# Routed expert blocks of 128 slots become pairs of 64-slot units, each with its own expert, in two column halves of the array

## The chip, the core and the metric

The kernel runs on one NeuronCore of one Trainium2 chip. Its engines each have an instruction queue of their own: TensorE (PE, matmuls; PEld its weight loads), VectorE (DVE), ScalarE (ACT), GpSimd (POOL) and SyncE (SP). SP computes nothing here: it issues nearly all DMA transfers, in program order. Engines wait for each other through semaphores. The metric is the device time of one execution in microseconds (us).

## The reference, cut to what matters

Two layers work on x, 1024 tokens of 256 features. Each adds a gated cross attention to x and then a gated mixture of experts. The attention does not change here. The mixture of experts is

```
x1       = layernorm(x)
combine  = top-k of 32 experts per token, with weights  # layer 0: 8 of 32, hidden width 176; layer 1: 6 of 32, width 96
routed   = sum over experts e: combine[:, e] * ((silu(x1 @ Wg[e]) * (x1 @ Wu[e])) @ Wd[e])
shared   = (silu(x1 @ sWg) * (x1 @ sWu)) @ sWd
x        = x + tanh(g) * (routed + shared)
```

All of it is in 32-bit floats. Only a token's own 8 (or 6) experts are computed: 8192 pairs of token and expert in layer 0, 6144 in layer 1.

## The kernel before, in words

**Routing.** VectorE finds for every token its experts and its place in each expert's segment of a DRAM buffer, `xs_dram` (32 segments). GpSimd scatters the normed rows there with indirect DMAs (L1723). Each segment is read in blocks of 128 slots. How full an expert gets is known only at run time, so the program holds a fixed number of blocks that is enough in the worst case, `BLOCKS` (L59): 95 in layer 0 and 79 in layer 1. `tables` (L1436) writes two rows of numbers for them into `tab`: where each block starts in `xs_dram`, and which expert it belongs to.

**One routed block**, in the order of its data:

1. SP loads the block's 128 rows into `xs` (L759), a ring of 8 buffers. In layer 0 it also loads the expert's down weights with two DMAs (L765), into `dn`, a ring of 8 buffers that lie in `oT` and `osb_v`. Start row and expert are read from `tab` into SP's registers four blocks at a time (`table_of`, L742 and L746).
2. PE transposes the rows (L948), and ACT copies them to `xTs` (L1199).
3. PE multiplies by the expert's gate and up weights (L982: contraction 256 in two halves, 352 output columns in layer 0, 192 in layer 1). All experts' gate and up weights lie in `W`, and a register picks the expert (`expert_in`, L956).
4. ACT applies silu (L1208), DVE multiplies (L1489), PE transposes the product (L994), DVE copies it to `hT` (L1500).
5. PE multiplies by the down weights (L1015). In layer 1 all down weights lie in `dn1`, next to the gate and up weights, and the expert is again picked by a register.
6. ACT scales the result (L1218), GpSimd scatters it to DRAM (L1733). To which row each slot goes, DVE works out for four blocks at a time (`goes_to`, L1502 to L1524).

A matmul of 32-bit floats shows as two instructions in the trace. The loop (`ffn` on each engine) is written out by hand: in step q PE transposes block q+1, multiplies gate and up of block q, transposes h of block q-1 and multiplies down of block q-2; a block has no loop counter at run time, every instruction is written out.

**Before and after.** Ahead of each layer's routed blocks stand 8 tiles of the shared expert (24 and 16 units in the same loop). SP starts the routed loads when all scatters have landed, and behind the last block it waits for all y scatters and reads the sums.

Of the kernel before, what the change touches and what calls it, by code (L numbers as in the profile page):

```python
# [21 lines left out]
P = 128  # L22
# [36 lines left out]
BLOCKS = tuple((T * k + EXPERTS * (P - 1)) // P for k in TOP)  # L59
# [4 lines left out]
XS_RING, Y_RING, Y2_RING, IDX, IDX_RING = 8, 4, 4, 4, 16  # L64
# [14 lines left out]
def build(nc, a):  # L79

    ctx = ExitStack()
    with ctx:
# [71 lines left out]
        junk = sb("junk", [P, 3, EXPERTS])  # L154
        bv = sb("bv", [P, 12])
        tab = sb("tab", [1, 2, 96], I32)
# [8 lines left out]
        row_no = sb("row_no", [P, 1])  # L165
        expert_no = sb("expert_no", [P, EXPERTS])
# [34 lines left out]
        with ExitStack() as prep:  # L201
# [18 lines left out]
        dn = [v[0:88, i * 2 * D:(i + 1) * 2 * D].rearrange("p (c n) -> p c n", c=2)  # L220
              for v in (oT[:, :, :].rearrange("p k t -> p (k t)"), osb_v[:, :]) for i in range(XS_RING // 2)]
# [8 lines left out]
        Wv = [W[:, 0:n * 2 * D].rearrange("p (j k g e r) -> p k g j e r", j=n, k=KD, g=2, e=EXPERTS) for n in (44, 24)]  # L230
        dn1 = W[0:96, 24 * 2 * D:24 * 2 * D + EXPERTS * D].rearrange("p (e n) -> p e n", e=EXPERTS)
# [81 lines left out]
        with nc.Block() as block:  # L313
            @block.sync
            def _(sp):
# [15 lines left out]
                for layer in range(2):  # L331
                    sp.dma_start(xs_dram[layer].rearrange("(e s) n -> s e n", s=SEG)[0:P],
                                 zeros[:, :].unsqueeze(1).to_broadcast([P, EXPERTS, ROW])).then_inc(padded[layer], 16)

            @block.gpsimd
            def _(pool):
# [33 lines left out]
                for layer in range(2):  # L370
                    k = TOP[layer]
                    pool.iota(token_row[:, layer, :], pattern=[[P * k, NT]], base=-1, channel_multiplier=k, **small)
                    step(pool.iota(dump_row[:, layer, :], pattern=[[P, Y_RING]], base=T * k, channel_multiplier=1, **small))
# [300 lines left out]
        def scatters(layer, u):  # L674
# [14 lines left out]
        dn_in = [sem(f"dn_in{i}") for i in range(XS_RING)]  # L689
# [3 lines left out]
            "xT_ps", "xT_sb", "g_ps", "s", "h", "hT_ps", "hT_sb", "down", "y_ps", "y_sb", "x_sh", "idx", "half", "pe_sum", "sum")}  # L693
# [15 lines left out]
        def all_scattered(layer, slot):  # L709

            return 16 * (len(range(slot, BLOCKS[0], Y_RING)) + layer * len(range(slot, BLOCKS[1], Y_RING)))

# [6 lines left out]
        with nc.Block() as block:  # L719
            @block.sync  # L720
            def _(sp):
# [17 lines left out]
                def table_of(layer, b):  # L739

                    n = min(IDX, BLOCKS[layer] - b)
                    _, rows = nc.values_load_multi_w_load_instructions(  # L742
                        tab[0:1, 0, b:b + n], engines=(mybir.EngineType.SP,), min_val=0, max_val=EXPERTS * SEG - P)
                    if layer == 1:
                        return [(r, None) for r in rows]
                    _, experts = nc.values_load_multi_w_load_instructions(  # L746
                        tab[0:1, 1, b:b + n], engines=(mybir.EngineType.SP,), min_val=0, max_val=EXPERTS - 1)
                    return list(zip(rows, experts))

                def block_in(layer, b, row, expert):  # L750
# [8 lines left out]
                    sp.dma_start(xs[:, slot, :], xs_dram[layer][bass.DynSlice(row, P), :]).then_inc(xs_in[slot], 16)  # L759
                    if layer == 0:  # L760
                        if b >= XS_RING:
                            sp.wait_ge(cf["down"], unit_of_block(b - XS_RING) + 1)
                        rows = wffn[0][SHARED[0]:, :, 2 * D:].rearrange("j (e c s) n -> j e c s n", e=EXPERTS, s=2)
                        for half in range(2):
                            sp.dma_start(dn[slot][half * TILES[0]:(half + 1) * TILES[0], :, :],  # L765
                                         rows[:, bass.DynSlice(expert, 1), :, half, :].rearrange("j e c n -> j (e c) n")
                                         ).then_inc(dn_in[slot], 16)

                def blocks_in(layer):

                    sp.wait_ge(cp["tab"], layer + 1)
                    table = table_of(layer, 0)
                    sp.wait_ge(scattered[layer], 16 * NT * TOP[layer])
                    for b in range(BLOCKS[layer]):
                        if b and b % IDX == 0:
                            table = table_of(layer, b)
                        block_in(layer, b, *table[b % IDX])
# [54 lines left out]
            def _(pe):  # L832
# [93 lines left out]
                def spread(layer):  # L926
# [5 lines left out]
                    for i in range(4):  # L932
                        last = pe.matmul(bank(7)[:, i * P:i * P + nb], rep[:, i, :], ident[:, 0:nb], start=True, stop=True)
                    last.then_inc(cp["rep_ps"], 1)

                def x_block_transposed(q):
# [4 lines left out]
                    pe.wait_ge(xs_in[slot], 16 * ring_turn(layer, b, XS_RING))  # L941
# [9 lines left out]
                def expert_in(q):  # L951

                    layer, _, b, _ = units[q]
                    if b == 0:
                        pe.wait_ge(cp["tab"], layer + 1)
                    _, of_block[q] = nc.values_load_multi_w_load_instructions(  # L956
                        tab[0:1, 1, b:b + 1], engines=(mybir.EngineType.PE,), min_val=0, max_val=EXPERTS - 1)

                def gate_up(q):
# [12 lines left out]
                    else:  # L972
# [7 lines left out]
                        pe.wait_ge(cf["xT_sb"], n + 1)  # L980
                        for k in range(KD):
                            last = pe.matmul(out, xTs[:, n % 2, k, :],  # L982
                                             Wv[layer][:, k, :, :, bass.DynSlice(of_block[q][0], 1), :],
                                             start=k == 0, stop=k == KD - 1)
# [12 lines left out]
                def down(q):  # L997
# [8 lines left out]
                    if kind == "routed" and layer == 0:  # L1006
                        pe.wait_ge(dn_in[index % XS_RING], 32 * (index // XS_RING + 1))
                    for c in range(parts):
                        if kind == "shared":
                            w = sw[:, part, 2 * D:]  # L1010
                        elif layer == 0:
                            w = dn[index % XS_RING][:, c, :]
                        else:
                            w = dn1[:, bass.DynSlice(of_block[q][0], 1), :].rearrange("p e n -> p (e n)")
                        last = pe.matmul(out, hT[0:rows, q % 2, c * P:(c + 1) * P], w, start=part == 0 and c == 0,  # L1015
                                         stop=ends(q) and c == parts - 1)
# [296 lines left out]
            def _(dve):  # L1313
# [122 lines left out]
                def tables(part, layer):  # L1436

                    nb = BLOCKS[layer]
                    if part == 0:
# [3 lines left out]
                        step(dve.tensor_scalar(nblk[:, :], count[:, :], 1.0 / P, 63.5 / P, ALU.mult, ALU.add))  # L1443
                        step(dve.tensor_scalar(nblk[:, :], nblk[:, :], ROUND, ROUND, ALU.add, ALU.subtract))
                        step(dve.tensor_tensor_scan(endb[:, :], ones[:, 0:EXPERTS], nblk[:, :], 0.0, ALU.mult, ALU.add))
                        before_it, own_count, nth, latest, rows = [bv[:, i:i + 1] for i in range(5)]
                        start, inside = bv[:, 5:6], bv[:, 6:7]
                        expert, lower, upper, row = [bv[:, i:i + 1] for i in range(8, 12)]
                        dve.scalar_tensor_tensor(junk[:, 0, :], endb[:, :], row_no[:, :], nblk[:, :], ALU.is_le, ALU.mult,
                                                 accum_out=before_it)  # L1450
                        step(dve.scalar_tensor_tensor(junk[:, 1, :], endb[:, :], row_no[:, :], ones[:, 0:EXPERTS], ALU.is_le,
                                                      ALU.mult, accum_out=expert))
                        dve.scalar_tensor_tensor(junk[:, 2, :], expert_no[:, :], expert, count[:, :], ALU.is_equal, ALU.mult,
                                                 accum_out=own_count)
                        dve.tensor_scalar(inside, expert, EXPERTS - 1.0, float(SEG), ALU.min, ALU.mult)
                        step(dve.tensor_scalar(nth, before_it, row_no[:, :], -1.0, ALU.subtract, ALU.mult))
                        dve.tensor_scalar(latest, own_count, -float(P), 0.0, ALU.add, ALU.max)
                        step(dve.tensor_scalar(rows, nth, float(P), None, ALU.mult))
# [4 lines left out]
                        dve.tensor_copy(rep[:, :, :], bv[:, 8:12].unsqueeze(2).to_broadcast([P, 4, P])).then_inc(cp["rep"], 1)  # L1463
                    else:
                        dve.wait_ge(cp["rep_ps"], layer + 1)
                        ps = bank(7)
                        dve.tensor_copy(tab[0:1, 0, 0:nb], ps[0:1, 3 * P:3 * P + nb])
                        dve.tensor_scalar(tab[0:1, 1, 0:nb], ps[0:1, 0:nb], EXPERTS - 1.0, None, ALU.min)
# [4 lines left out]
                        step(dve.tensor_scalar(low[:, 0:nb], ps[:, P:P + nb], row_no[:, :], None, ALU.is_le))  # L1473
                        dve.scalar_tensor_tensor(filled[:, 0:nb], ps[:, 2 * P:2 * P + nb], row_no[:, :], low[:, 0:nb],
# [26 lines left out]

                def goes_to(layer, b, part):  # L1502
# [7 lines left out]
                    elif part == 1:  # L1510
                        for i in range(b, b + n):
                            dve.wait_ge(xs_in[i % XS_RING], 16 * ring_turn(layer, i, XS_RING))
# [20 lines left out]
                def ffn(layer, i):  # L1533
# [85 lines left out]

                for s in range(STEPS):  # L1620
# [264 lines left out]
```

## Time and profile before

| | |
|---|---|
| time, median of 3 runs | 890.02 us (890.01 to 892.17) |
| span of the profiled execution, from its first to its last instruction | 931.3 us |
| routed blocks of layer 0, first gate matmul to last down matmul | 352.5 to 595.4 us |
| routed blocks of layer 1, the same | 762.3 to 902 us |
| busy share of the span: PE, DVE, ACT, POOL | 80%, 58%, 47%, 52% |

The profiled execution was longer than the timed ones; nothing is given of what lies around its span. The rows of its trace are shown further down. In them, PE, DVE, ACT and POOL rows are instructions at work, and SPq rows are DMA issues in SP's queue.
### The profile page before, as it was taken

Reading aid. Unit: us, or ns where it says so; the run is one execution under the profiler, and the core shown is the slowest. Engines: PE = TensorE matmul, PEld = TensorE weight load, DVE = VectorE, ACT = ScalarE, POOL = GpSimd, SP = SyncE. Lnnn points to the kernel's source line nnn. Section 1 sums busy time; section 2 is a strip of 40 time slices with the busy share of each in tenths; the row PEclk is TensorE's granted clock in tenths of the full one; section 3 lists DMA queues with packets and bytes.
Section 4 is the critical chain, followed back from the end, with each engine's and each line's share of the span. In section 5 each row is a group of like instructions: output and inputs, shape, how many; then the busy total and the mean of one; then the engine's idle time right before and its main releaser. Section 6 shows DMA issues by size and latency. Waiting matters only on the chain.

```text
span 931.3 us, 20204 instructions
## 1 busy us (share of the span) xinstructions
PE 741.2 (80%) x5678; PEld 544.3 (58%) x5719; DVE 535.8 (58%) x1323; ACT 437.5 (47%) x1058; POOL 480.9 (52%) x530
## 2 busy tenths in 40 slices
PE   6657777767687878999999999548856579999974
PEld 4535455544455665677777777425545467777753
DVE  5989879789784533344344444277653444444435
ACT  3568776666663112444444444236633015555540
POOL 3817665787886551333433433375246535555550
PEclk9869875775857798999999999857877789999997
DMA  8909999999999945656666666378026435555538
GB/s 281 371 10 184 172 164 193 177 216 216 202 187 248 331 159 174 189 182 198 197 188 199 191 187 198 138 281 299 16 77 176 152 114 180 167 171 172 159 108 313
DMA packets 222085, 175.53 MB, mean 188 GB/s; under 512 B 146698, under 2 KB 200922, under 8 KB 220954
## 3 DMA queue, kind: packets, MB, share of 16 engines
q1 hardware_dynamic: 207978, 132.52, 56.2%
q0 software_dynamic: 13728, 41.17, 12.3%
q8 instruction: 52, 0.85, 0.4%
q14 instruction: 55, 0.45, 0.2%
q10 hardware_dynamic: 272, 0.52, 0.1%
HBM read 87.92 MB, written 52.69 MB: 151 GB/s over the span
## 4 chain that ended last, share of the span: by engine, by line
PE 42%; issue 11%; POOL 11%; DVE 11%; DMA 10%; ACT 3%; SPq 3%; another core or an unknown queue 2%; POOLq 0%; DVEq 0%; ACTq 0%
PE psum L982 15%; PE psum L1015 11%; DMA pT<-p 6%; POOL p L1710 3%; POOL xs_dram L1723 3%; PE psum L994 3%; DVE nmax L1321 3%; PE psum L948 3%; POOL y_dram L1733 3%; PE psum L970 2%; DMA W<-y_dram 2%; PE psum L841 2%; ACT e L1169 1%; SPq L765 1%
## 5 line engine op out<-in xcount | busy, mean ns | idle before, releaser
L1733 POOL DMA_INDIRECT y_dram<-ybuf,idxi x174 | 167.4, 962 | 232.7 <-ACT ybuf L1218 186.7
L1500 DVE COPY hT<-psum 88x256 f32<-88x256 f32 (+2 forms) x214 | 74.2, 347 | 214.6 <-PE psum L994 103.0
L982 PE MATMUL psum<-W,xTs 128*128 x696 | 196.0, 405 | 0.7 <-issue 0.7
L1169 ACT ACTIVATE e<-psum,nmax 128x1024 f32<-128x1024 f32 x128 | 142.4, 1115 | 57.6 <-DVE nmax L1321 40.6
L1710 POOL TENSOR_SCALAR p<-e 128x1024 f16<-128x1024 f32 x128 | 133.9, 1046 | 65.6 <-ACT e L1169 38.9
L1321 DVE TENSOR_REDUCE nmax<-psum 128x1 f32<-128x1024 f32 x128 | 152.3, 1219 | 20.5 <-PE psum L841 17.3
L1723 POOL DMA_INDIRECT xs_dram<-xaug,posi x112 | 110.3, 985 | 69.2 <-issue 31.9
L1208 ACT ACTIVATE sg<-psum 128x176 f32<-128x176 f32 (+2 forms) x214 | 61.1, 286 | 161.9 <-PE psum L982 82.4
L1218 ACT ACTIVATE ybuf<-psum,dot 128x256 f32<-128x256 f32 x174 | 82.6, 474 | 110.3 <-PE psum L1015 100.9
L982 PEld LDWEIGHTS psum<-W,xTs 128*128 128x128 f32 x696 | 115.9, 193 | 23.2 <-issue 2.9
L841 PE MATMUL psum<-kstack,qstack 128*128 128x512 bf16 x215 | 93.2, 511 | 40.4 <-ACT e L1169 33.2
L854 PEld LDWEIGHTS psum<-osb_v,pT 128*128 128x128 f16 x1024 | 66.7, 104 | 53.5 <-DMA pT<-p 37.9
L994 PE MATMUL psum<-ident,h 128*88 128x128 f32 (+2 forms) x309 | 71.2, 281 | 23.4 <-DVE h L1492 12.3
L854 PE MATMUL psum<-osb_v,pT 128*128 128x16 f16 x1024 | 71.4, 175 | 19.0 <-DMA pT<-p 17.8
L948 PE MATMUL psum<-ident,xs 128*128 128x128 f32 x348 | 68.4, 278 | 13.4 <-DMA xs<-xs_dram 13.3
L1199 ACT ACTIVATE xTs<-psum 128x256 f32<-128x256 f32 x174 | 65.7, 378 | 22.3 <-PE psum L948 21.9
L994 PEld LDWEIGHTS psum<-ident,h 128*88 128x88 f32 (+2 forms) x309 | 39.0, 128 | 62.3 <-issue 20.6
L948 PEld LDWEIGHTS psum<-ident,xs 128*128 128x128 f32 x348 | 49.7, 144 | 32.4 <-DMA xs<-xs_dram 14.9
L855 PE MATMUL psum<-osb_v,unlift 128*128 128x16 f16 x1024 | 68.4, 172 | 0.0
L855 PEld LDWEIGHTS psum<-osb_v,unlift 128*128 128x128 f16 x1024 | 61.9, 103 | 10.6 <-issue 7.4
L1489 DVE TENSOR_TENSOR h<-sg,psum 128x176 f32<-128x176 f32 (+1 forms) x174 | 67.0, 385 | 1.7 <-ACT sg L1208 1.1
L1015 PE MATMUL psum<-W,hT 96*128 x158 | 54.4, 426 | 0.2
(223 smaller groups left out, 1140.9 us busy)
## 6 DMA issues: line engine op xcount, KB each, us to landing
xs<-xs_dram SPq DMA_DIRECT2D x174, 160.0 KB
W<-in_wffn SPq DMA_DIRECT2D x15, 1024.0 KB, 14.8
xs_dram<-zeros SPq DMA_DIRECT2D x2, 5120.0 KB, 25.6
oT<-in_wffn SPq DMA_DIRECT2D x96, 88.0 KB
osb_v<-in_wffn SPq DMA_DIRECT2D x94, 88.0 KB
W<-y_dram SPq DMA_DIRECT2D x6, 1024.0 KB, 6.7
W<-y_dram SPq DMA_DIRECT2D x8, 768.0 KB, 9.2
W<-in_wffn SPq DMA_DIRECT2D x4, 768.0 KB
```

Of the source, the lines that this page charges most:

```text
L841: last = pe.matmul(bank(s_bank(s) + n), qstack[:, t // TH, head, t % TH * P:(t % TH + 1) * P], kstack[:, head, n * BANK:(n + 1) * BANK], s ...
L854: pe.matmul(out, pT[:, s % PT_RING, k, :], v, start=k == 0, stop=False)
L855: last = pe.matmul(out, unlift[:, :], v, start=False, stop=k == NT - 1)
L948: last = pe.transpose(ps[:, k * P:(k + 1) * P], xs[:, slot, k * P:(k + 1) * P], ident[:, :])
L982: last = pe.matmul(out, xTs[:, n % 2, k, :], Wv[layer][:, k, :, :, bass.DynSlice(of_block[q][0], 1), :], start=k == 0, stop=k == KD - 1)
L994: last = pe.transpose(bank(4)[0:rows, c * P:(c + 1) * P], h[:, q % 2, c * rows:(c + 1) * rows], ident[:, :])
L1015: last = pe.matmul(out, hT[0:rows, q % 2, c * P:(c + 1) * P], w, start=part == 0 and c == 0, stop=ends(q) and c == parts - 1)
L1169: act.activation(e[:, s % E_RING, :], bank(s_bank(s), 2), ACT.Exp, bias=nmax[:, s % S_RING:s % S_RING + 1], accum_out=esum[:, t, head:head ...
L1321: dve.tensor_reduce(nmax[:, s % S_RING:s % S_RING + 1], bank(s_bank(s), 2), AX.X, ALU.max, negate=True).then_inc(c2["max"], 1)
L1710: pool.tensor_scalar(p16[:, s % P_RING, :], e[:, s % E_RING, :], PMAX, LIFT, ALU.mult, ALU.add).then_inc(c2["p16"], 1)
L1723: pool.indirect_dma_start(xs_dram[layer][:, :], bass.IndirectOffsetOnAxis(posi[:, t, k:k + 1], 0), xaug[:, t, :], None).then_inc(scattered ...
L1733: pool.indirect_dma_start(y_dram[layer][:, :], bass.IndirectOffsetOnAxis(idxi[:, slot:slot + 1], 0), ybuf[:, b % Y_RING, :], None).then_in ...
```

## The change

A block is now a pair of units of 64 slots (`SUB`, `SR`). Slots 0 to 63 belong to the first unit, slots 64 to 127 to the second, each with a start row and an expert of its own. `BLOCKS` becomes 80 in layer 0 and 64 in layer 1. The core of the diff:

```diff
+SUB, HALF = (2, 2), P // 2
+SR = tuple(P // n for n in SUB)
-BLOCKS = tuple((T * k + EXPERTS * (P - 1)) // P for k in TOP)
+BLOCKS = tuple(-(-((T * k + EXPERTS * (r - 1)) // r) // n) for k, r, n in zip(TOP, SR, SUB))
-XS_RING, Y_RING, Y2_RING, IDX, IDX_RING = 8, 4, 4, 4, 16
+XS_RING, DN_RING, DN2_RING, Y_RING, Y2_RING, IDX, IDX_RING = 8, 4, 3, 4, 4, 4, 16
...
+        def down_in(queue, b, j, expert):
+            slot = b % DN_RING
+            for half in range(2):
+                queue.dma_start(dn[slot][half * TILES[0]:(half + 1) * TILES[0], j, :, :],
+                                rows[:, bass.DynSlice(expert, 1), :, half, :].rearrange("j e c n -> j (e c) n")
+                                ).then_inc(dn_in[slot], 16)
...
                 def table_of(layer, b):
-                        tab[0:1, 0, b:b + n], engines=(mybir.EngineType.SP,), min_val=0, max_val=EXPERTS * SEG - P)
+                    rows = [nc.values_load_multi_w_load_instructions(
+                        tab[0:1, 0, j, at], engines=(mybir.EngineType.SP,), min_val=0, max_val=EXPERTS * SEG - SR[layer])[1]
+                        for j in range(SUB[layer])]
...
+                    return rows, list(zip(*[nc.values_load_multi_w_load_instructions(
+                        tab[0:1, 1, j, at], engines=(mybir.EngineType.SP,), min_val=0, max_val=EXPERTS - 1)[1]
+                        for j in range(SUB[0])]))
...
-                    sp.dma_start(xs[:, slot, :], xs_dram[layer][bass.DynSlice(row, P), :]).then_inc(xs_in[slot], 16)
+                    for j in range(SUB[layer]):
+                        sp.dma_start(xs[j * n:(j + 1) * n, slot, :],
+                                     xs_dram[layer][bass.DynSlice(rows[j], n), :]).then_inc(xs_in[slot], 16)
+                def downs_in(b, experts):
+                    if b >= DN_RING:
+                        sp.wait_ge(cf["down"], unit_of_block(b - DN_RING) + 1)
+                    for j in range(SUB[0]):
+                        down_in(sp, b, j, experts[j])
...
+                        block_in(layer, b, [r[b % IDX] for r in rows])
+                        if layer == 0 and b >= IDX:
+                            downs_in(b - IDX, earlier[b % IDX])
...
                 def gate_up(q):
+                        pe.wait_ge(cf["gu2"], n + 1)
                         for k in range(KD):
-                            last = pe.matmul(out, xTs[:, n % 2, k, :],
+                            pe.matmul(out[0:HALF, :], xTs[:, n % 2, k, 0:HALF],
                                              Wv[layer][:, k, :, :, bass.DynSlice(of_block[q][0], 1), :],
-                                             start=k == 0, stop=k == KD - 1)
+                                      start=k == 0, stop=k == KD - 1, skip_group_check=True)
+                            last = pe.matmul(out[HALF:P, :], xTs[:, n % 2, k, HALF:P], gu2[layer][n % 2][:, k, :],
+                                             start=k == 0, stop=k == KD - 1, skip_group_check=True)
...
+                def second_gate_up(q):
+                    dve.wait_ge(cf["g_ps"], q - 1)
+                    dve.tensor_copy(gu2[layer][n % 2].rearrange("p k (g j r) -> p (k g) j r", g=2, r=ROWS),
+                                    Wkg[layer][:, :, :, bass.DynSlice(expert, 1), :].rearrange("p c j e r -> p c j (e r)")
+                                    ).then_inc(cf["gu2"], 1)
+                def second_down(q):
+                    dve.tensor_copy(dn2[b % DN2_RING], dn1[:, bass.DynSlice(expert, 1), :].rearrange("p e n -> p (e n)")
+                                    ).then_inc(cf["dn2"], 1)
...
                     if q < end:
                         hidden(q)
+                    if q + 2 < end and routed(q + 2):
+                        second_gate_up(q + 2)
+                    if layer == 1 and q < end and routed(q):
+                        second_down(q)
```

Gate and up of a block are now four matmuls of 64 stationary columns instead of two of 128, and down likewise (four instead of two in layer 0, two instead of one in layer 1); the first unit's output goes to partitions 0 to 63, the second's to 64 to 127. The first unit's weights are read where they lie; for the second unit VectorE copies the expert's gate and up weights into `gu2` (in `xT`, two buffers), and in layer 1 the down weights into `dn2` (three buffers). In layer 0 SP loads the down weights of both units, in a ring of 4 blocks where it was 8, four blocks behind the rows. The zero fill of `xs_dram` at the start covers 64 rows per expert instead of 128, and `tables` works out two units per block.

In SP's queue, where layer 0 goes from one group of four blocks to the next (L742 and L746 read start rows and experts, L759 loads rows, L765 down weights), stood before:

```order
L742 TENSOR_LOAD tab
L742 ISA x8
L746 TENSOR_LOAD tab
L746 ISA x8
L759 ISA
L759 DMA xs<-xs_dram 128x320
L765 ISA
L765 DMA osb_v<-in_wffn 44x2x256
L765 ISA
L765 DMA osb_v<-in_wffn 44x2x256
```

At the same place now (L774 and L779 read the tables, L794 loads rows, L741 down weights, of which four such DMAs follow instead of two):

```order
L774 TENSOR_LOAD tab
L774 ISA x8
L774 TENSOR_LOAD tab
L774 ISA x8
L779 TENSOR_LOAD tab
L779 ISA x8
L779 TENSOR_LOAD tab
L779 ISA x8
L794 ISA
L794 DMA xs<-xs_dram 64x320
L794 ISA
L794 DMA xs<-xs_dram 64x320
```

A block thus went from three DMAs to six in this queue, and a group of four blocks from two table reads with 16 register operations to four with 32.

On PE, one step of layer 0's loop stood before as follows (L982 gate and up, L956 the next block's expert, L994 the transposes of h, L1015 down, L948 the transposes of the next rows):

```order
L982 ISA
L982 MATMUL psum<-W,xTs 128x352
L982 ISA
L982 MATMUL psum<-W,xTs 128x352
L956 TENSOR_LOAD tab
L956 ISA x2
L994 MATMUL psum<-ident,h 88x128 x2
L1015 MATMUL psum<-oT,hT 128x256 x2
L948 MATMUL psum<-ident,xs 128x128 x2
```

And now (L1028 and L1031 are the halves of gate and up, L1069 and L1071 those of down):

```order
L1028 ISA
L1028 MATMUL psum<-W,xTs 64x352
L1031 MATMUL psum<-xT,xTs 64x352
L1028 ISA
L1028 MATMUL psum<-W,xTs 64x352
L1031 MATMUL psum<-xT,xTs 64x352
L1001 TENSOR_LOAD tab
L1001 ISA x2
L1042 MATMUL psum<-ident,h 88x128 x2
L1069 MATMUL psum<-oT,hT 64x256
L1071 MATMUL psum<-oT,hT 64x256
L993 MATMUL psum<-ident,xs 128x128 x2
```

The transposes stay whole, so each step goes from the whole array to the halves and back twice.

## Rows read from the trace of the kernel before

**Rows 1.** The page's first line.

```profile
span 931.3 us, 20204 instructions
```

**Rows 2.** Stretches: busy us of PE, PEld, DVE, ACT, POOL; granted clock; DMA share; GB/s.

```profile
60.00:290.00 230.00, 171.17 (x2440) 114.16 (x2479) 195.53 (x282) 159.72 (x276) 171.11 (x173) 0.69 1.03 183
352.50:592.40 239.90, 237.04 (x1130) 174.31 (x1130) 101.19 (x310) 99.89 (x281) 88.22 (x92) 0.99 0.60 185
762.30:902.00 139.70, 132.05 (x713) 104.09 (x712) 62.53 (x260) 75.75 (x235) 73.36 (x77) 0.99 0.52 160
```

**Rows 3.** The chain that ended last: start us, us, what.

```profile
389.36 1.19 PE psum L982 x4
...
583.68 1.19 PE psum L982 x4
...
758.65 2.28 DMA xs<-xs_dram
```

**Rows 4.** PE in time, one step of layer 0: start us, us, line, operation.

```profile
450.37 1.03 PE L1015 MATMUL psum<-oT,hT 88*128 88x256 f32 x4
...
451.23 0.38 PE L948 MATMUL psum<-ident,xs 128*128 128x128 f32 x2
...
451.45 1.35 PE L982 MATMUL psum<-W,xTs 128*128 x4
```

**Rows 5.** SP's queue in time, layer 0, four blocks from one table read on.

```profile
457.34 0.35 SPq L759 DMA_DIRECT2D xs<-xs_dram  x1
...
458.94 0.36 SPq L759 DMA_DIRECT2D xs<-xs_dram  x1
459.50 0.77 SPq L765 DMA_DIRECT2D osb_v<-in_wffn  x2
...
463.01 0.77 SPq L765 DMA_DIRECT2D osb_v<-in_wffn  x2
467.05 0.35 SPq L759 DMA_DIRECT2D xs<-xs_dram  x1
```

**Rows 6.** SP's instructions of L742, L746, L765: min/median/max ns, first and last start.

```profile
L742 SPq FUSED_REGOPS  x174: 3/151/725, 329.7 to 885.0; - x174
L742 SPq TENSOR_LOAD <-tab x44: 108/556/927, 328.8 to 883.8; - x44
L746 SPq TENSOR_LOAD <-tab x24: 127/304/687, 331.2 to 573.9; - x24
L765 SPq DMA_DIRECT2D oT<-in_wffn x96: 17/296/1230, 348.7 to 571.8; - x96
L765 SPq DMA_DIRECT2D osb_v<-in_wffn x94: 16/296/1938, 358.1 to 580.6; - x94
```

**Rows 7.** What SP's queue waited for: us in total, times, longest.

```profile
SPq L759 <- DMA xs_dram<-xaug,posi: 25.1, 2, 15.4
SPq L765 <- PE psum L1015: 2.1, 5, 0.7
```

**Rows 8.** PE in time, attention of layer 1, groups of 32 columns.

```profile
641.35 0.66 PE L1061 MATMUL psum<-ident,W 128*128 128x128 f32 x4 [0.28 <-ACT osb_v L1259]
641.94 1.07 PE L1074 MATMUL psum<-osb_v,ctxT 128*32 128x256 f32 x16
642.83 0.62 PE L1082 MATMUL psum<-ident,a1rs 128*32 128x128 f32 x16
```

**Rows 9.** PE in time, layer 1, gate and up of two blocks.

```profile
867.27 0.81 PE L982 MATMUL psum<-W,xTs 128*128 x4
...
868.80 0.81 PE L982 MATMUL psum<-W,xTs 128*128 x4
```

**Rows 10.** DVE by line and shape: count, busy us, mean ns.

```profile
L1568 DVE TENSOR_TENSOR W<-W 128x768 f32<-128x768 f32 x5 | 4.8, 957 | 14.8 <-DMA W<-y_dram 14.8
L1463 DVE COPY rep<-bv 128x512 f32<-128x512 f32 x2 | 0.9, 426 | 0.1
```

**Rows 11.** The last down matmuls of layer 0 on PE (first and last start).

```profile
L1015 PE MATMUL psum<-osb_v,hT x188: 377/379/382, 371.9 to 595.0; 88*128 88x256 f32 x188
```

More of the change, by code:

```diff
@@ L692, in build @@
         cf = {n: sem("cf_" + n) for n in (
-            "xT_ps", "xT_sb", "g_ps", "s", "h", "hT_ps", "hT_sb", "down", "y_ps", "y_sb", "x_sh", "idx", "half", "pe_sum", "sum")}
+            "xT_ps", "xT_sb", "g_ps", "s", "h", "hT_ps", "hT_sb", "down", "y_ps", "y_sb", "x_sh", "idx", "half", "pe_sum", "sum", "gu2", "dn2")}
         cx = {n: sem("cx_" + n) for n in (
@@ L758, in block_in @@
                         sp.wait_ge(cf["idx"], done_before(layer, b, XS_RING))
-                    sp.dma_start(xs[:, slot, :], xs_dram[layer][bass.DynSlice(row, P), :]).then_inc(xs_in[slot], 16)
[L760 to L767, printed above, removed]
+                    n = SR[layer]
+                    for j in range(SUB[layer]):
[6 more added lines that the diff above has]
+                        down_in(sp, b, j, experts[j])
                 def blocks_in(layer):
                     sp.wait_ge(cp["tab"], layer + 1)
-                    table = table_of(layer, 0)
+                    rows, experts = table_of(layer, 0)
                     sp.wait_ge(scattered[layer], 16 * NT * TOP[layer])
@@ L775, in blocks_in @@
                         if b and b % IDX == 0:
-                            table = table_of(layer, b)
-                        block_in(layer, b, *table[b % IDX])
+                            earlier = experts
+                            rows, experts = table_of(layer, b)
+                        block_in(layer, b, [r[b % IDX] for r in rows])
+                        if layer == 0 and b >= IDX:
+                            downs_in(b - IDX, earlier[b % IDX])
+                    for b in range(BLOCKS[0] - IDX, BLOCKS[0]):
+                        if layer == 0:
+                            downs_in(b, experts[b % IDX])
                 def sums_in(layer, t):
@@ L932, in spread @@
                     for i in range(4):
-                        last = pe.matmul(bank(7)[:, i * P:i * P + nb], rep[:, i, :], ident[:, 0:nb], start=True, stop=True)
+                        pe.matmul(bank(7)[:, i * nb:(i + 1) * nb], rep[:, i, :], ident[:, 0:nb], start=True, stop=True)
+                    for j in range(1, SUB[layer]):
+                        at = j * SR[layer]
+                        last = pe.matmul(bank(7)[0:1, (3 + j) * nb:(4 + j) * nb], rep[:, 3, at:at + 1], ident[:, 0:nb],
+                                         start=True, stop=True)
                     last.then_inc(cp["rep_ps"], 1)
@@ L1447, in tables @@
[L1447 to L1452, printed above, removed]
@@ L1453, in tables @@
-                        dve.scalar_tensor_tensor(junk[:, 2, :], expert_no[:, :], expert, count[:, :], ALU.is_equal, ALU.mult,
-                                                 accum_out=own_count)
+                        before_it, own_count, nth, latest, rows, start, inside = [bv[:, i, 0:n] for i in range(7)]
+                        expert, lower, upper, row = [bv[:, i, 0:n] for i in range(8, 12)]
+                        no = unit_no[:, layer, 0:n]
+                        for j in range(n):
+                            dve.scalar_tensor_tensor(junk[:, 3 * j, :], endb[:, :], no[:, j:j + 1], nblk[:, :], ALU.is_le,
+                                                     ALU.mult, accum_out=before_it[:, j:j + 1])
+                            last = dve.scalar_tensor_tensor(junk[:, 3 * j + 1, :], endb[:, :], no[:, j:j + 1],
+                                                            ones[:, 0:EXPERTS], ALU.is_le, ALU.mult,
+                                                            accum_out=expert[:, j:j + 1])
@@ L1455, in tables @@
+                        step(last)
+                        for j in range(n):
+                            dve.scalar_tensor_tensor(junk[:, 3 * j + 2, :], expert_no[:, :], expert[:, j:j + 1], count[:, :],
+                                                     ALU.is_equal, ALU.mult, accum_out=own_count[:, j:j + 1])
                         dve.tensor_scalar(inside, expert, EXPERTS - 1.0, float(SEG), ALU.min, ALU.mult)
-                        step(dve.tensor_scalar(nth, before_it, row_no[:, :], -1.0, ALU.subtract, ALU.mult))
```

122 lines of the change are left out of this document (85 added, 37 removed).

## The prediction

> **What bounds the kernel now.** I read the stretches first, then the chain that ended last, then the queues in time. The profiled execution spans 931.3 us [rows 1], 41 us more than the median of the timed runs; the sums below are made against it and are scaled at the end by 890.02 / 931.3 = 0.956. In the routed blocks of layer 0 TensorE is busy for 237 of 240 us at a granted clock of 0.99, the full 2.4 GHz; in those of layer 1 for 132 of 140 us [rows 2]. Both are bound by TensorE. The chain shows the beat: 79 rows of L982 from 389.36 to 583.68 us [rows 3], so 194.32 / 78 = 2.49 us a block, with nothing late. 95 blocks at 2.49 are 237 us. So the number of blocks is worth cutting, if a block stays as cheap.
>
> The reader should then look at who comes second, and that is SP. In one group of four blocks it goes from rows load to rows load in 457.34 to 458.94 = 1.60 us, of which the rows load takes 0.56 up to the first down DMA, and the two down DMAs the other 1.04 [rows 5]. At the group's end a down pair starts at 463.01 and the next rows load at 467.05: 4.04 us in place of 1.04, so the two table reads take 3.0 us [rows 5]. Four blocks are then 4 x 1.60 + 3.0 = 9.4 us, against TensorE's 4 x 2.49 = 9.96. SP was at 94% of its limit, and waited for TensorE at the down ring five times for 2.1 us in all [rows 7]. This queue gets the most added work.
>
> **The change part by part.**
>
> Blocks: 15 fewer in each layer. If everything kept pace, 15 x 2.49 = 37 us less in layer 0, and 15 x 1.77 = 27 in layer 1 (139.7 us for 79 blocks [rows 2]).
>
> SP in layer 0: six DMAs a block for three. A DMA costs about 0.5 us of the queue (1.60 / 3 = 0.53; a down DMA 1.04 / 2 = 0.52, with the ring waits in it) [rows 5], so a block takes 6 x 0.5 = 3.0 us. I take no discount for a rows load of 64 rows: the 88-row down DMA, with half the bytes, costs as much. The table reads double: four loads and 16 values for two and 8, so 6.0 us a group. Four blocks become 4 x 3.0 + 6.0 = 18 us, or 4.5 us a block. The first group's tables are read while SP waits for the scatters (25.1 us in two waits over both layers [rows 7]), so the queue needs 80 x 3.0 + 19 x 6.0 = 354 us. Bounds: the same sum for before, 95 x 1.60 + 23 x 3.0 = 221 us, stands against 232 us measured (348.7 to 580.6 [rows 6]); some of the rest was waiting, but if all of it was slow steps, it is 354 x 1.05 = 372. From below, the bare instructions without the gaps: six times 0.30 is 1.8 us a block, and a group's tables 2 x 0.56 + 2 x 0.30 + 16 x 0.15 = 4.1 [rows 6], in all 80 x 1.8 + 19 x 4.1 = 222 us; I go by the starts, since the gaps are there in every row of the queue. The down ring of 4 holds nothing back at this pace.
>
> So SP takes the beat in layer 0. It starts at 348 as now; its last down DMA leaves at 348 + 354 = 702, lands 2.3 us later (a rows load took 2.28 [rows 3]), and the last down matmuls take 0.9 (450.37 to 451.23 [rows 4]): 705 us for 595.4 now [rows 11]. Layer 0: **+110 us**, bounds -9 (SP at 222 us leaves the beat to TensorE, first rival) and +128.
>
> TensorE's block. Halves side by side should cost what the whole array did: in the attention of layer 1, 16 matmul instructions of 256 columns in four groups of 32 columns took 641.94 to 642.83 = 0.89 us [rows 8], as long as 4 on the whole array (0.87 [rows 4]). What is added is the change of shape. From L948 to L982 the next group starts 451.23 + 0.38 - 451.45 = 0.16 us ahead of the modelled end [rows 4], from L1061 (whole) to L1074 (quarters) only 641.35 + 0.66 - 641.94 = 0.07 [rows 8]: 0.09 us a change, four a block, 0.36. A block of layer 0 is 2.85 us, below SP's 4.5, and hidden. In layer 1 two L982 groups are 867.27 to 868.80 = 1.53 us apart [rows 9], and become 1.89. If the halves cost nothing, 1.53; if they don't run side by side, the second rival.
>
> VectorE's copies. A float copy of 512 elements took 426 ns, an add of 768 took 957 [rows 10]; if the copy runs at twice the add's rate, that is 160 ns and 0.52 ns an element. A copy of 704 then takes 0.53 us (0.89 at the add's rate), of 384 0.36 (0.56), of 256 0.29 (0.43). VectorE was busy 101.2 / 95 = 1.07 us a block in layer 0 and 62.5 / 79 = 0.79 in layer 1 [rows 2], so 1.6 and 1.44, with some 0.4 for its own table reads (3.0 / 2 a group of four [rows 5]): 2.0 and 1.8. Hidden under 4.5 in layer 0; level with TensorE in layer 1, and above it (2.1) at the slow rate. The copy for block q+2 stands ahead of `goes_to` and of the next hT copy; TensorE needs it two steps later.
>
> Layer 1. SP: two DMAs and half the table work, 2 x 0.5 + 3.0 / 4 = 1.75 us. TensorE 1.89, VectorE 1.8. Before, the largest was 1.53 and a block took 1.77, 0.24 more. I take 1.89 + 0.24 = 2.13: 64 x 2.13 = 136 us for 140. **-4 us**, bounds -19 (64 x 1.89) and +10 (VectorE 2.1 + 0.24).
>
> The rest. The halved zero fill at the start lies beside prologue work that nobody waits for it in, and `tables` lengthens by some ten VectorE instructions under the same wait for the scatters: 0, at most 2 us either way.
>
> Sum: 931.3 + 110 - 4 = 1037, scaled 992. If what stretches the profiled execution lies outside layer 0's TensorE-bound stretch, it is in the queues, and 354 us shrinks with them by 41 / (931 - 237) = 6%, to 333: then 890 + 110 - 21 - 4 = 975. I forecast **985 us**.
>
> **The rivals.**
>
> First, on the other side: SP's steps don't set the beat, because outside the profile they are shorter, or overlap the transfers. TensorE would then set it: 80 x 2.85 = 228 for 237, -9; with layer 1 between -4 and -19, 903 to 918, scaled **870 us**. It decides from SP at 2.85 us a block instead of 4.5. For it: the lower bound above (222 us), and odd starts in the queue 0.07 us apart after a stall (shortest L765 record 16 ns [rows 6]). Against it: the queue runs in order, its tables are register work that no transfer hides, and a 41 us stretch in 931 is far from the 37% needed. The Trainium skill (DMA: Bandwidth & Descriptors, Issuing engines are not separate DMA queues) says that the time a sequencer takes to start a DMA is usually small relative to the DMA. By that rule this rival would win. The trace agrees for one load, 0.56 us to start and 2.28 to land, but not for a queue of six starts a block.
>
> Second, the two halves run one after the other: gate and up 1.19 us more, down 0.87, so 2.85 + 2.06 = 4.9 us in layer 0 (392 us) and 1.89 + 0.65 + 0.43 + 0.24 = 3.2 in layer 1 (205): +148 and +65, 1144, scaled **1094**. Against it [rows 8].
>
> Third, the clock. While SP reads tables, TensorE starves for some 6 us in 18, and could fall to 1.2 GHz: 2 x 2.49 + 0.4 = 5.4 us a block, 432 us, +188 - 4, 1115, scaled **1066**. For it: 60 to 290 us, busy for 74%, got 0.69 [rows 2]. Against it: at half clock TensorE would be the slowest and never idle, and both routed stretches, nearly always busy, had 0.99 [rows 2]. The Trainium skill (TensorE: Matmul & The Clock Gate, HAM oscillation) describes such bursts between DMA waits running at the low level each time; by it this rival gains.
>
> **How the numbers follow.** Forecast 0.77, first rival 0.10, second 0.05, third 0.08. Its own uncertain terms (SP's step, the share of the stretch) put the forecast between 925 and 1030; to leave out no more than 2 in 10, the range is 910 to 1050 us. What changes by less than 0.3% can't be told from no change here. Faster: 0.08, nearly all of the first rival; within 0.3%: 0.02, at the point between it and the forecast; slower: 0.90.
>
> **What would show it.** In the profile after, SP's queue in layer 0 without waits, rows loads of whole groups about 18 us apart, and TensorE idle before down (now waiting for the `oT` and `osb_v` loads), busy for some 65%. L1028 and L1031 should overlap, four instruction pairs in about 1.2 us. In layer 1 a block of 2.0 to 2.3 us. Wrong: rows loads that wait for TensorE in layer 0, L1031 starting where L1028 ends, or layer 0's stretch staying near 240 us.

## The result, and the profile after

The changed kernel takes 1062.85 us (median of 4 runs, 1061.86 to 1079.34) against 890.33 for the kernel before on the same chip: a ratio of 1.191, 95% interval 1.185 to 1.198. Forecast were 985 us, range 910 to 1050. The sign was right; the size was not, by 78 us.

The execution whose trace the prediction read was a slower one than the timed ones (931.3 us for 890), and the kernel before was therefore recorded again. The page's first line of that second recording:

```profile
span 888.7 us, 20204 instructions
```

Its stretches, columns as in [rows 2] (layer 0's routed blocks, what lies between the layers, layer 1's routed blocks):

```profile
341.00:587.00 246.00, 241.60 (x1145) 177.53 (x1145) 102.15 (x312) 101.43 (x284) 89.77 (x93) 0.98 0.59 182
587.00:734.40 147.40, 97.29 (x717) 71.18 (x715) 89.56 (x269) 60.47 (x195) 83.74 (x98) 0.79 0.53 185
734.40:859.50 125.10, 124.77 (x715) 103.32 (x716) 61.78 (x260) 78.59 (x236) 73.13 (x77) 0.99 0.59 182
```

Kernel after, the page's first line and its row of granted clock (a digit for each fortieth of the span, in tenths of full speed), then the same three stretches:

```profile
span 1061.0 us, 22779 instructions
...
PEclk9878967566599788887888888888579988789998
```

```profile
347.00:738.50 391.50, 299.98 (x1603) 124.09 (x1603) 118.78 (x340) 87.06 (x239) 75.00 (x79) 0.84 0.44 133
738.50:884.00 145.50, 95.85 (x719) 71.21 (x717) 90.63 (x278) 60.39 (x195) 83.60 (x98) 0.81 0.54 187
884.00:1032.20 148.20, 140.31 (x965) 69.45 (x965) 80.98 (x336) 64.28 (x191) 59.40 (x62) 0.91 0.41 125
```

| stretch, us | before, first trace | before, second trace | after |
|---|---|---|---|
| up to the first routed block | 350 | 341 | 347 |
| layer 0, routed | 245 | 246 | 392 |
| between the layers | 166 | 147 | 146 |
| layer 1, routed | 141 | 125 | 148 |
| end | 29 | 29 | 29 |

So against the second trace layer 0 grew by 146 us and layer 1 by 23, the rest by about 4: 173 us, as timed. What the first trace had too much lay outside layer 0 (9 + 19 + 16 us); what caused it stays open.

What holds layer 0 is read from SP's queue, the counterpart of [rows 5] (start us, us, line; x2 and x4 are the DMAs of one block):

```profile
493.45 1.14 SPq L794 DMA_DIRECT2D xs<-xs_dram  x2
...
496.88 1.14 SPq L794 DMA_DIRECT2D xs<-xs_dram  x2
498.22 1.83 SPq L741 DMA_DIRECT2D oT<-in_wffn  x4
500.28 1.14 SPq L794 DMA_DIRECT2D xs<-xs_dram  x2
...
505.40 1.83 SPq L741 DMA_DIRECT2D osb_v<-in_wffn  x4
513.09 1.16 SPq L794 DMA_DIRECT2D xs<-xs_dram  x2
...
533.15 1.19 SPq L794 DMA_DIRECT2D xs<-xs_dram  x2
```

A block is 496.88 to 500.28 = 3.40 us, 1.34 of it for the two row loads and 2.06 for the four down DMAs; the tables take 505.40 to 513.09 less 2.06 = 5.63. A group of four comes every 19.64 and 20.06 us. In all of layer 0 the view of SP's waits is empty: the queue never stood still. Who waits are the others; these two waits are 91 of the 92 us in which TensorE was idle in layer 0 (us in total, times, longest):

```profile
PE psum L1069 <- DMA oT<-in_wffn: 68.9, 19, 4.6
PE psum L1042 <- DVE h L1554: 22.3, 18, 2.1
```

The halves do run side by side. One TensorE step, where its clock was high:

```profile
505.50 0.44 PE L993 MATMUL psum<-ident,xs 128*128 128x128 f32 x2
505.87 0.51 PE L1028 MATMUL psum<-W,xTs 128*64 x1
505.87 0.51 PE L1031 MATMUL psum<-xT,xTs 128*64 128x352 f32 x1
506.21 0.46 PE L1028 MATMUL psum<-W,xTs 128*64 x1
506.22 0.46 PE L1031 MATMUL psum<-xT,xTs 128*64 128x352 f32 x1
```

The matmuls of the two halves start 10 ns apart or less, and four pairs take 505.87 to about 507.3 = 1.4 us, where four matmuls on the whole array took 1.35 [rows 4]. VectorE's copies cost what was estimated (0.53, 0.36 and 0.29 us), and VectorE itself waits for the row loads (L1608, 173 us in layer 0):

```profile
L1582 DVE COPY xT<-W 128x704 f32 x80 | 40.7, 509 | 24.3 <-issue 24.3
L1582 DVE COPY xT<-W 128x384 f32 x64 | 22.6, 353 | 21.3 <-PE psum L1031 18.3 <-PE psum L1015 1.8 <-issue 1.2
L1594 DVE COPY xT<-W 96x256 f32 x64 | 18.6, 290 | 0.0
```

### The profile page after: what moved, and what is told of

Same layout as the page of the kernel before. It is cut to its first block, busy times and chain, and to the rows that moved or that the text cites. A ratio compares the mean times of both kernels' runs of the same rounds, so it can differ in the third digit from the quotient of the medians.

```text
span 1061.0 us, 22779 instructions
## 1 busy us (share of the span) xinstructions
PE 798.1 (75%) x6391; PEld 450.9 (43%) x6432; DVE 571.9 (54%) x1445; ACT 411.5 (39%) x968; POOL 458.1 (43%) x508
## 4 chain that ended last, share of the span: by engine, by line
issue 41%; POOL 19%; PE 11%; DVE 10%; DMA 8%; ACT 3%; SPq 1%; POOLq 0%; DVEq 0%; ACTq 0%
POOL y_dram L1833 12%; DMA pT<-p 4%; POOL p L1810 3%; DVE nmax L1377 3%; PE psum L1015 3%; POOL xs_dram L1823 2%; ACT e L1225 2%; DMA W<-y_dram 2%; PE psum L1060 1%; PE psum L1028 1%; DMA xs<-xs_dram 1%; PE psum L882 1%; DVE a1nb L1685 1%; PE psum L1042 1%; ACT W L1299 1%
## 5 line engine op out<-in xcount | busy, mean ns | idle before, releaser
L1833 POOL DMA_INDIRECT y_dram<-ybuf,idxi x144 | 138.8, 964 | 417.4 <-ACT ybuf L1274 408.1
L1031 PE MATMUL psum<-xT,xTs 128*64 128x352 f32 (+1 forms) x576 | 199.3, 475 | 0.0
L1028 PE MATMUL psum<-W,xTs 128*64 x576 | 199.2, 476 | 0.0
L1274 ACT ACTIVATE ybuf<-psum,dot 128x256 f32<-128x256 f32 x144 | 68.3, 474 | 244.2 <-PE psum L1071 243.6
L1565 DVE COPY hT<-psum 88x256 f32<-88x256 f32 (+2 forms) x184 | 63.6, 346 | 149.2 <-PE psum L1042 103.1
L1608 DVE TENSOR_TENSOR both<-xs,own 128x256 f32<-128x256 f32 x36 | 15.2, 422 | 181.4 <-DMA xs<-xs_dram 181.3
L1069 PE MATMUL psum<-oT,hT 88*64 88x256 f32 x160 | 58.2, 500 | 68.9 <-DMA oT<-in_wffn 68.9
L1028 PEld LDWEIGHTS psum<-W,xTs 128*64 128x64 f32 x576 | 75.8, 153 | 65.2 <-issue 61.1
L1582 DVE COPY xT<-W 128x704 f32 (+1 forms) x144 | 63.3, 439 | 45.6 <-issue 25.5
L1031 PEld LDWEIGHTS psum<-xT,xTs 128*64 128x64 f32 x576 | 75.8, 153 | 0.0
```

Source lines behind the costliest of these rows:

```text
L1028: pe.matmul(out[0:HALF, :], xTs[:, n % 2, k, 0:HALF], Wv[layer][:, k, :, :, bass.DynSlice(of_block[q][0], 1), :], start=k == 0, stop=k == ...
L1031: last = pe.matmul(out[HALF:P, :], xTs[:, n % 2, k, HALF:P], gu2[layer][n % 2][:, k, :], start=k == 0, stop=k == KD - 1, skip_group_check= ...
L1833: pool.indirect_dma_start(y_dram[layer][:, :], bass.IndirectOffsetOnAxis(idxi[:, slot:slot + 1], 0), ybuf[:, b % Y_RING, :], None).then_in ...
```

## The experiments

The theory: SP's issue queue sets the beat, and only its price per step was too low. The rivals: TensorE with its clock and its changes of shape sets it; the landing of the transfers sets it. The kernels without "before" in their name start from the kernel after. Stage times below are from their traces, in the stretches of the table above.

**The kernel before, again.**

> The kernel before, unchanged. It tells where the 41 us lie between its profiled span (931.3) and its timed median (890), which the kernel after does not have (1061.0 and 1062.85). If the shown profile fell on a disturbed execution, its span now comes out near 890, and the layer 0 blocks' spacing (2.49 us) or the middle stage is shorter in it. If recording slows this kernel down, the span is near 931 again while the timed runs stay at 890.

Median 893.96, and 891.01 for the other copies of it on that chip; the new trace spans 888.7 us. The first alternative holds.

**One DMA for a unit's down weights.**

```diff
-            for half in range(2):
-                queue.dma_start(dn[slot][half * 44:(half + 1) * 44, j, :, :], rows[:, expert, :, half, :]...)
+            queue.dma_start(dn[slot][:, j, :, :], a["wdn0"][expert]...)
```

> The kernel after, with a unit's down weights loaded by one DMA of 88 rows in place of two of 44 (the host stores the same weights in that order); 4 DMAs on SP per block in place of 6, the same bytes. Theory (SP's issue queue sets layer 0's beat, 19.8 us for four blocks): 8 steps of 0.49 us less in a group of four, 15.9 us, 80 blocks give -78 us: 985 us (970 to 1000). Rival 1 (the clock that falls in TensorE's gaps and its own changes of shape set the beat): no change beyond 10 us, 1053 to 1063. Rival 2 (landing of the transfers or their bytes set it): the same bytes in fewer descriptors, within 10 us as well.

999.68 us. Layer 0 fell from 392 to 319 us (-73; 78 expected) with the same bytes. Layer 1, whose code is untouched, was 155 us here for 148, which is half of the gap to 985. In this run TensorE was granted 0.50 of its clock there for 41 us (848.8 to 889.8; in the kernel after only for some 17 us, below), and SP waited 12.8 us in all for 3.8.

**SP's table values without bounds checks.**

```diff
   tab[0:1, 0, j, at], engines=(SP,), min_val=0, max_val=EXPERTS * SEG - SR[layer],
+  skip_runtime_bounds_check_because="..."        # and the same for the experts
```

> The kernel after, with the run-time bounds check left out of SP's reads of the row and expert tables (16 values per four blocks; a register operation of 0.147 us and an assert behind each value, 0.25 us from one to the next). No DMA changes. Theory (SP's queue sets the beat): 4.0 us less in a group of four of 19.8, -80 us in layer 0: 983 us (970 to 1000). Rivals 1 and 2 (TensorE with its clock; the transfers): within 10 us of 1063.

975.02 us. No transfer differs, and layer 0 took 316 us (-76), layer 1 132 (-16). Stretches of layer 0 and 1, and who SP waits for in layer 1:

```profile
347.00:663.00 316.00, 272.31 (x1605) 115.75 (x1605) 118.84 (x340) 85.92 (x239) 75.26 (x78) 0.91 0.55 166
...
811.00:943.00 132.00, 130.80 (x963) 66.38 (x965) 80.08 (x336) 63.38 (x191) 59.09 (x62) 0.98 0.46 140
```

```profile
SPq L790 <- DVE h L1556: 17.5, 17, 1.5
```

In the kernel after the same view of layer 1 had

```profile
SPq L788 <- DVE h L1554: 3.8, 3, 1.7
```

So SP's queue was the bound in layer 1 too, if only just: 1.34 us for two row loads and half of the table work, 5.63 / 8, are 2.04 us a block, and TensorE needs 2.00 (below). SP issued the row loads of layer 1 up to 1019.5 us, 135.5 us from the stretch's start at 884.0, with only those 3.8 us of waiting; its sum is 64 x 2.04 = 131. The last blocks took the other 12.7 us. With the checks gone, SP waits for the engines again, and TensorE sets the beat: 64 x 2.00 + 4 = 132.

One stretch of layer 1 of the kernel after ran at the low clock level, 1.2 GHz; in the 12 us ahead of it TensorE had been busy for 9.8:

```profile
905.00:917.00 12.00, 9.83 (x75) 4.84 (x73) 6.81 (x28) 4.87 (x15) 4.93 (x5) 1.00 0.43 131
917.00:934.50 17.50, 17.50 (x78) 7.52 (x76) 7.20 (x32) 5.45 (x15) 4.80 (x5) 0.51 0.38 116
```

Its blocks took 3.53 us each and not 2.00. As SP was the bound and waited 3.8 us in all, this can have cost about that much at most (an estimate from these waits).

**Both.**

> Both edits together. Theory: SP's group of four would be 19.8 - 3.9 - 4.0 = 11.9 us, 2.97 us per block, under TensorE's own 3.07 us per block (a stretch of the kernel after in which nothing was missing). So TensorE takes the beat: layer 0 about 80 x 3.07 = 246 us in place of 391, 918 us in all (900 to 940); SP's relief is worth less here than the sum of the two (158). If the two gains add up fully (905 and below), TensorE's block is shorter than 3.07. Rival 1: near 1060.

908.65 us, ratio to before 1.024 (1.015 to 1.034). Layer 0 249.7 us, layer 1 131.6. The two gains, 63 and 88, add up to 151 and gave 154, but the two kernels with one edit differ in layer 1 (155 and 132 us); in layer 0 alone 73 and 76 add up to 149 and gave 142. There TensorE waits for nothing from 400 to 580 us, and SP now waits for TensorE at the down ring:

```profile
SPq L739 <- PE psum L1070: 9.7, 7, 2.1
```

TensorE's block is 3.07 us:

```profile
510.94 0.44 PE L992 MATMUL psum<-ident,xs 128*128 128x128 f32 x2
511.31 0.51 PE L1027 MATMUL psum<-W,xTs 128*64 x1
...
512.25 0.46 PE L1027 MATMUL psum<-W,xTs 128*64 x1
...
512.64 0.42 PE L1041 MATMUL psum<-ident,h 128*88 128x128 f32 x2
512.99 0.43 PE L1068 MATMUL psum<-osb_v,hT 88*64 88x256 f32 x1
...
513.69 0.38 PE L1068 MATMUL psum<-osb_v,hT 88*64 88x256 f32 x1
...
514.01 0.44 PE L992 MATMUL psum<-ident,xs 128*128 128x128 f32 x2
514.37 0.51 PE L1027 MATMUL psum<-W,xTs 128*64 x1
```

From L992 to L1027 pass 0.37 us; with whole-array work on both sides it was 451.45 - 451.23 = 0.22 [rows 4]. Four changes of shape are 3.07 - 2.49 = 0.58 us, 0.15 each on average. They show on the way into the halves (the 0.15 just named) and on the way back: the transposes of h start 0.39 us behind the last pair of gate and up, where before one instruction of L982 took 1.19 / 4 = 0.30 [rows 3], and those of the next rows 0.32 behind the last pair of down, for 0.86 / 4 = 0.22 [rows 4]. With the loads out of the way the change itself does not pay: 80 x 3.07 = 246 for 95 x 2.49 = 237, and in layer 1, with 2.00 us per block in the median, 64 x 2.00 = 128 for 79 x 1.53 = 121.

**Control: both edits on the kernel before.**

> Control: the kernel before with the same two edits on SP (one DMA of 88 rows for a block's down weights; no bounds checks on SP's table values). SP's group of four falls from 9.7 us to about 9.7 - 4 x 0.35 - 8 x 0.25 = 6.3 us, but TensorE's 2.49 us per block (9.96 a group) stays. Theory (whoever has the longest queue per block sets the beat, TensorE in the kernel before): within 8 us of 891. If the two edits are gains in themselves, whatever bounds the kernel: 40 to 100 us faster.

891.76 us, ratio 0.9986 (0.9954 to 1.0019). The time that SP is spared turns into waiting for TensorE at the down ring of layer 0 (6.9 us in the second trace of before):

```profile
SPq L765 <- PE psum L1014: 100.7, 85, 2.2
```

The same edits that gave 154 us give nothing where TensorE sets the beat.

**The price of a row load by its shape.**

```diff
+ XS_CUT = ((128,), (64, 64), (96, 32), ("cols",), (112, 16), (80, 48), (88, 40), (32, 32, 64))   # by ring slot
```

> The kernel before, its load of 128 rows cut in another way in each of the eight ring slots: 128; 64+64; 96+32; two column halves of 128 rows; 112+16; 80+48; 88+40; 32+32+64. What SP pays for each is read from its rows. If the row count sets it, the 64-row loads take 0.47 us again and the column halves about 0.30 to 0.36; if it is the second load from the same rows or into the same tile that is dear, the column halves and the second pieces of every cut take 0.47. Some 0.5 us more on SP per block lift its beat from 2.43 to about 2.9 us over TensorE's 2.49: by the theory layer 0 grows by some 40 us (25 to 60), 930 us in all; if SP's queue did not matter, within 8 us of 891.

957.27 us (one run), for 930 expected; layer 0 300.5, +55 against the second trace of before (25 to 60 expected), and layer 1 +11, which the expectation left out. SP's queue (each x2 or x1 is one block's load), then the two column halves by line (min/median/max ns):

```profile
511.55 0.35 SPq L772 DMA_DIRECT2D xs<-xs_dram  x1
...
513.16 1.16 SPq L772 DMA_DIRECT2D xs<-xs_dram  x2
...
515.62 0.33 SPq L772 DMA_DIRECT2D xs<-xs_dram  x1
516.15 0.33 SPq L772 DMA_DIRECT2D xs<-xs_dram  x1
...
526.36 0.87 SPq L772 DMA_DIRECT2D xs<-xs_dram  x2
```

```profile
L769 SPq DMA_DIRECT2D xs<-xs_dram x44: 348/357/1385, 345.7 to 911.6; - x44
```

The first row is 128 rows, then 64+64, 96 and 32, 80+48. The pair of 64s takes 1.16 us from its first start to its last end, a pair of 80 and 48 0.87. The other pieces (16, 32, 40, 48, 80, 88, 96, 112 and 128 rows, and column halves of 128) all took 0.30 to 0.36 us in the median; of the row counts tried only 64 took 0.49, wherever it stood. So neither "fewer rows" nor "the second load" is the reason. Why 64 is dear stays open.

**TensorE's step in another order, then the second unit's down loads on ScalarE's queue.**

```diff
   x_block_transposed(q + 1)
+  h_transposed(q - 2)
   gate_up(q)
-  h_transposed(q - 1)
-  down(q - 2)
+  down(q - 3)            # ScalarE's and VectorE's steps follow by one
```

> The kernel after with one down DMA per unit and no bounds checks, and TensorE's step put in another order: x transposes of the next block, h transposes of the block two back (one back before), then gate/up halves and the down halves of the block three back, so that the array changes its shape twice per step and not four times. At 0.143 us per change TensorE's block would be 3.07 - 0.29 = 2.78 in layer 0 and 1.72 in layer 1. SP needs 2.96 per block in layer 0 (11.83 us for a group of four in the kernel with both edits), so it sets the beat there: 80 x 2.96 = 237 + 4 (-9); layer 1 64 x 1.72 + 4 = 114 (-18): about 882 us (870 to 895). If the changes of shape cost nothing and 3.07 is the halves' own time: 908 as before the reordering.

> The same, with the second unit's down weights issued from ScalarE's queue (a table read per four blocks and one DMA per block there), so that SP needs about 2.3 us per block. Theory: TensorE's 2.78 us sets layer 0: 222 + 4 us (-24 against both edits without the reordering), layer 1 114 (-18): 866 us (855 to 880), 2 to 4% faster than the kernel before. If ScalarE, which then has some 1.7 us per block and whose copies and silu stand behind the DMA, becomes late: 885 to 905.

925.70 and 921.83 us: slower than without the reordering, and both expectations missed. A block without a stall did what was said, 2.79 us in layer 0 and 1.71 in layer 1. But in layer 0 every fourth block took 0.6 to 1.9 us more, and in layer 1 two of every four took some 0.4 and 1.0 us more. Waits of layer 0 in the second kernel, VectorE's and TensorE's:

```profile
DVE both L1631 <- DMA xs<-xs_dram: 26.0, 19, 4.5
```

```profile
PE psum L1040 <- DVE hT L1588: 23.4, 19, 4.9
```

With down one step later, the ring of down buffers came free one step later, SP issued its row loads behind that wait (in the first of the two kernels it waited there 32 times, 25.7 us in all, for 7 times and 9.7 us without the reordering), and VectorE's step for the next four blocks (`both`) waited for them with the next hT copy behind it, 19 times. In layer 1 the same rhythm came with VectorE's table read (four values with their checks).

**Those stalls removed.** Down loads six blocks behind the row loads on SP, not four, and VectorE's read without checks; with all loads on SP, and with the second unit's down loads on ScalarE.

> The kernel 'reorder' (all loads on SP) with two stalls of four-block rhythm taken out: VectorE's read of the second unit's experts without bounds checks (about 1 us of register work less in each group of four), and the down loads issued six blocks behind the row loads in place of four, so that VectorE's step that needs the next group's rows finds them landed (it waited 26 us for them in layer 0). Theory: SP's 2.96 us per block then sets layer 0, 80 x 2.96 + 4 = 241 (260.5 before), layer 1 64 x 1.71 + 4 = 114 (138): about 882 us (870 to 895). If the stalls come from something else (VectorE's own work, its copies of weights among it): above 905.

> The same with the second unit's down weights on ScalarE's queue. Theory: TensorE's 2.79 us per block is all that is left in layer 0, 80 x 2.79 + 4 = 227 (256 in 'reorder_act'), layer 1 114 (140): about 867 us (855 to 880), faster than the kernel before by 1.5 to 4%. If VectorE, whose copies and reads stand at about 2.3 us per block, is the new bound: 885 to 915.

895.53 us (ratio 1.003, 1.000 to 1.006) and 880.64 (0.986, 0.981 to 0.990), each just above its range. Layer 0 came to 242.6 and 229.0 us as expected, one bound by SP, one by TensorE. The wait for the row loads in the second kernel is gone:

```profile
DVE both L1634 <- DMA xs<-xs_dram: 1.9, 1, 1.9
```

Layer 1 fell from 138 and 140 us to 125 in both, still 11 above the expectation.

**TensorE's expert read once in four blocks.**

> The kernel 'final_act' with TensorE's read of the first unit's expert made once in four blocks, without bounds checks, in place of once in each block. In 'final_act' layer 1 runs at 1.90 us per block (125.6 us) and not at the 1.71 that TensorE's rows need; its queue holds a table load of 0.53 to 0.62 us and some 0.4 us of register work per block ahead of the down halves' weights. If that holds layer 1 back: 64 x 0.15 to 0.19 us less, layer 1 at 113 to 117, 870 us in all (862 to 876). If VectorE holds it back (h, hT, two copies and a quarter of the four-block work, about 1.75 us per block): within 4 us of 'final_act', 877 to 884.

871.96 us, ratio 0.975 (0.971 to 0.979): faster than both kernels. Layer 1 went from 125.6 to 117.6 us at 1.71 us a block, so TensorE's own queue had held it. Its stretches, and one step of layer 0:

```profile
347.00:577.30 230.30, 227.31 (x1604) 118.10 (x1605) 124.64 (x340) 93.17 (x239) 75.66 (x78) 0.99 0.75 227
577.30:726.00 148.70, 98.40 (x721) 71.77 (x717) 91.28 (x278) 60.39 (x196) 83.53 (x98) 0.79 0.52 183
726.00:843.60 117.60, 115.67 (x963) 71.05 (x965) 84.72 (x336) 63.53 (x191) 63.73 (x61) 0.97 0.53 157
```

```profile
499.59 0.51 PE L1034 MATMUL psum<-W,xTs 128*64 x1
...
501.79 0.44 PE L994 MATMUL psum<-ident,xs 128*128 128x128 f32 x2
502.06 0.38 PE L1048 MATMUL psum<-ident,h 128*88 128x128 f32 x2
502.38 0.51 PE L1034 MATMUL psum<-W,xTs 128*64 x1
```

A step is 499.59 to 502.38 = 2.79 us with two changes of shape for four: 2.49 + 2 x 0.15. The edits of this last kernel that touch TensorE's and VectorE's table reads were not tried on the kernel before.

## Why the prediction was right about the sign and wrong about the size

- **SP takes the beat in layer 0: right.** The empty view of its waits, the idle time ahead of `down` and the two relief edits (-73 and -76 us in layer 0, no TensorE instruction touched) show it; the control shows that the edits are worth nothing elsewhere. The first rival, that SP's steps don't set the beat, is out. The Trainium skill (DMA: Bandwidth & Descriptors, Issuing engines are not separate DMA queues) calls the time to start a DMA usually small relative to the DMA; it holds for one DMA here (0.56 us to start and 2.28 to land in the kernel before), but not for six in a row per block, which cost 3.40 us of SP's queue, with 1.41 of table reads beside them.
- **The failed step is SP's term, +110, which measured +146.** "I take no discount for a rows load of 64 rows" looked only for a discount. The two row loads take 1.34 us and not 1.0, the four down DMAs 2.06 and not 2.0, so a block is 3.40 us for 3.0. The tables were near (5.63 for 6.0). The sum 80 x 3.40 + 19 x 5.63 = 379 us, with some 10 us of single slow steps, is the measured 343.0 to 732.6 = 390, for 354. The upper bound of 372 was a spread over the steps of before and did not contain a step of a new shape.
- **The term of layer 1, -4, which measured +23, failed twice.** Its base, 1.77 us a block, came from the first trace (the second has 125.1 / 79 = 1.58). And SP was put at 1.75 us; with its dear row loads it needs 2.04, over TensorE's 2.00 (forecast 1.89). Measured are 148.2 / 64 = 2.32 a block, with the last blocks and SP's waits in it. Without SP's checks layer 1 fell from 148 to 132.
- **The scaling by 0.956 failed.** It spread the 41 us over everything and took some 45 us off the sum (1037 to 992; the product is 991). None of them lay in layer 0: 28 lay in stretches that the change hardly touches and 16 in the base of layer 1. The difference belonged on the timed median unscaled. 890 + 110 - 4 = 996, and the two mis-sized terms, 36 and 27, with some 4 us elsewhere make it 1063.
- **Halves side by side: right, the second rival is out.** A change of shape costs 0.15 us on average for 0.09 estimated. The Trainium skill (TensorEngine Tiling (Array Packing), Key Properties) says that changing the tiling mode drains TensorE, without a price; the trace shows the price, 0.15 us, and not what TensorE does in it.
- **The third rival's 1066 us was near the result by chance.** The clock did fall between the bursts (0.84 in layer 0, and the slices of the page's row of granted clock there stand at 7 or 8), but the time followed SP's queue, which waited for no engine there: with the table checks gone the granted clock was still 0.91, and layer 0 took 316 us with SP's groups of four 15.6 us apart in the median, 80 x 3.9 = 312. What the clock cost shows at most in layer 1, some 4 us in the stretch at 0.51.

## What to carry to other kernels

Count an in-order issuing queue like a compute engine: instructions per block times their measured start-to-start time, register reads and bounds checks with them, and compare it with the engine that sets the beat now; the queue that is second today can be the bound after a change that cuts the block count and doubles its work. Price a new transfer shape with an interval open to both sides, since its cost to issue need not follow its size. Look for the part of a trace in which a profiled execution is longer than the timed median before scaling by it.

## What the runs showed of the hardware that was not expected

- A DMA of exactly 64 rows of 1,280 bytes took SP 0.49 us to issue (0.47 in the kernel after); nine other row counts from 16 to 128 took 0.30 to 0.36 (medians).
- The bounds check of one value read from a table into SP's registers costs 0.25 us of the queue: without the checks of its 16 values a group of four fell from 19.7 to 15.6 us (medians).
- TensorE pays 0.15 us on average when it goes from whole-array work to two column halves or back; ordering the step so that like work is adjacent took 0.28 us off a block of 3.07.
